# The product of ek and v on GpSimd instead of VectorE, one identity tile for all stages, and another head for the first mixing stage

## The reference

```
h   = layernorm(x) @ Wqkv + bqkv                    # 16 heads of 32
o   = softmax(q k^T / sqrt(32) + alibi bias) v
x   = x + o @ Wout + bout
emb = layernorm(x) + ctx
q, k, v = emb @ wq + bq, emb @ wk + bk, emb @ wv + bv
ek  = exp(k - max_t k);  ew = exp(w - max w)        # w: pos_bias within 128 of the diagonal, else 0
y   = sigmoid(q) * (ew @ (ek * v)) / (ew @ ek)
a   = layernorm(y @ wo + bo + emb) ...              # then a dense block of 512 -> 2048 -> 512 with relu
x   = x + layernorm(relu(a @ w1 + b1) @ w2 + b2 + a)
x   = x + quantised feed-forward with a depthwise convolution(layernorm(x))
```

## Time and profile before

| | |
|---|---|
| median of 3 runs | 3562.73 us (3561.97 to 3564.03) |
| the profiled execution | 3561.91 us |
| its span in the profile | 3560.3 us |
| PE busy | 3177.0 us, 89% |
| DVE busy | 2358.0 us, 66% |
| ACT busy | 1769.2 us, 50% |
| POOL busy | 1127.6 us, 32% |
| mean granted TensorE clock | 0.957 |

### The profile page before, as it was taken

How to read it: one execution, slowest core, us unless ns; L and a number is a source line. 1 busy time by engine, 2 the same in 40 slices (tenths; PEclk the granted TensorE clock), 3 DMA queues, 4 the chain that set the end, 5 groups by cost and what they waited for, 6 DMA issues and landing times. The chain is left out here.

```text
span 3560.3 us, 57155 instructions
## 1 busy us (share of the span) xinstructions
PE 3177.0 (89%) x19234; PEld 2286.5 (64%) x19234; DVE 2358.0 (66%) x4214; ACT 1769.2 (50%) x3131; POOL 1127.6 (32%) x892
## 2 busy tenths in 40 slices
PE   6998999999999999689996898599999999467887
PEld 5776666666666666467775777477887888334443
DVE  5562888888888888555553788634445444379996
ACT  3331888888888888412222222132222222066662
POOL 2343222311321231143331355311111111058886
PEclk9999999999999999889997999799999999689999
DMA  6775212211311222355644443321111110201112
GB/s 216 242 244 166 67 57 74 77 60 56 91 60 57 69 80 64 123 188 187 226 167 155 135 142 124 101 95 42 42 42 43 42 41 30 80 23 54 60 42 71
DMA packets 239608, 350.54 MB, mean 98 GB/s; under 512 B 31792, under 2 KB 129104, under 8 KB 239440
## 3 DMA queue, kind: packets, MB, share of 16 engines
q1 hardware_dynamic: 208784, 291.46, 25.3%
q0 software_dynamic: 8640, 31.77, 2.7%
q10 hardware_dynamic: 22016, 25.17, 2.0%
HBM read 210.68 MB, written 137.64 MB: 98 GB/s over the span
## 5 line engine op out<-in xcount | busy, mean ns | idle before, releaser
L863 DVE CUSTOM_DVE_ANT_0 attend_scores<-attend_scores,attend_bias_table 128x1024 f32<-128x1024 f32 x512 | 630.4, 1231 | 164.0 <-PE attend_scores L717 157.7
L790 ACT ACTIVATE attend_probs<-attend_scores,attend_neg_max 128x1024 f32<-128x1024 f32 x512 | 571.2, 1116 | 136.9 <-DVE attend_neg_max L863 126.8
L729 PE MATMUL attend_turned<-attend_ident,attend_probs 128*128 128x128 f32 x4096 | 557.5, 275 | 11.5 <-DVE attend_probsT L871 11.2
L729 PEld LDWEIGHTS attend_turned<-attend_ident,attend_probs 128*128 128x128 f32 x4096 | 473.0, 141 | 121.4 <-DVE attend_probsT L871 27.2
L717 PE MATMUL attend_scores<-attend_k_stack,attend_q_stack 96*128 96x512 f32 x1024 | 375.2, 448 | 14.4 <-DMA attend_q_stack<-qk_parts 9.8
L798 ACT COPY attend_probsT<-attend_turned 128x512 f32<-128x512 f32 x640 | 359.1, 583 | 25.4 <-PE attend_turned L729 23.5
L2207 DVE TENSOR_TENSOR cross_ffn_h_lo<-cross_ffn_hidden,cross_ffn_h_hi 128x512 fp32r<-128x512 f32 x128 | 96.3, 757 | 361.9 <-ACT cross_ffn_h_hi L2104 361.3
L691 POOL TENSOR_TENSOR attend_out_parts<-attend_out_full,attend_out_parts 128x256 fp32r<-128x256 f32 x64 | 46.5, 727 | 856.7 <-ACT attend_out_parts L805 856.7
L744 PE MATMUL attend_out_acc<-attend_probsT,attend_v_in 128*32 128x256 f32 x4096 | 312.9, 389 | 0.7 <-DVE attend_out_full L881 0.7
L871 DVE COPY attend_probsT<-attend_turned 128x512 f32<-128x512 f32 x384 | 263.4, 686 | 1.3 <-PE attend_turned L729 1.3
L717 PEld LDWEIGHTS attend_scores<-attend_k_stack,attend_q_stack 96*128 96x128 f32 x1024 | 154.1, 190 | 171.4 <-issue 169.2
(11 more groups left out here) (302 smaller groups left out, 6630.0 us busy)
## 6 DMA issues: line engine op xcount, KB each, us to landing
qk_parts<-qkv_qk_out SPq DMA_DIRECT2D x64, 512.0 KB, 3.2
attend_k_stack<-qk_parts SPq DMA_DIRECT2D x192, 128.0 KB, 2.5
attend_q_stack<-qk_parts SPq DMA_DIRECT2D x192, 128.0 KB, 2.6
qkv_wq_raw<-L_ffn_w POOLq DMA_DIRECT2D x16, 1024.0 KB, 7.8
o_parts<-attend_out_parts ACTq DMA_DIRECT2D x64, 256.0 KB, 2.5
mix_in_o_in<-o_parts SPq DMA_DIRECT2D x32, 512.0 KB, 6.7
qkv_x_in<-x SPq DMA_DIRECT2D x8, 1024.0 KB, 6.0
v_rows<-qkv_v_out SPq DMA_DIRECT2D x32, 256.0 KB, 3.4
```

Source lines behind the costliest of these rows:

```text
L729: last = pe.transpose(turned[:, x, c], probs[:, i % 2, k * P:(k + 1) * P], ident[:, :])
L790: act.activation(probs[:, i % 2], scores[:, i % 2], ACT.Exp, bias=neg_max[:, i % 4:i % 4 + 1], scale=-1.0, accum_out=den[:, qg % 2, j, h:h ...
L863: dve.tensor_tensor_reduce(scores[:, i % 2], scores[:, i % 2], bias_table[:, h, at:at + T], -1.0, BIG, ALU.add, ALU.min, neg_max[:, i % 4: ...
```

## The change

Four things are done together.

1. **The product of ek and v.** The four instructions leave VectorE's odd step and stand at the end of GpSimd's odd step, behind `mask_band`, `bias_x` and `embed`. VectorE keeps the sums and waits for each product (`ekv_ready`).
2. **One identity.** It is made once, in `project_qkv`, in a tile of the whole program. The five later stages take it and lose their memset, their select and TensorE's wait for them.
3. **Wout, o_in, x_in and the output bias go ahead.** They live in tiles that attention and `mix_in` share (`carried`). GpSimd issues the loads of Wout and of the bias as its first instructions of `attend` and splits Wout behind the tables of turn 0. SP loads `x_in` and `o_in` of half 0 behind the last turn's loads. GpSimd adds the bias to `x_in` before attention's last two low parts.
4. **The head of `mix_in`.** SP starts with the context, wk and wv. TensorE waits for nothing before its first products. VectorE does `residual_norm(0)` first and splits wk, wv and wq behind it. The wait for the four remaining bias loads comes late on every engine.

```diff
@@ attend, SP, behind the turns
+                def load_first():
+                    sp.wait_ge(wout_step, 2)
+                    sp.dma_start(first["x_in"][:, :, :], half_of(x, 0)).then_inc(x_loaded, 16)
+                    sp.wait_ge(out_stored, KB * G * 16)
+                    for g in range(KB):
+                        sp.dma_start(first["o_in"][:, g].bitcast(F32), o_parts[0, g, :, :, 0:HALF]).then_inc(first_loaded, 16)
+
                 turns(sp, body)
+                load_first()
+                sp.wait_ge(first_loaded, KB * 16)
@@ attend, GpSimd
+                pool.dma_start(first["x_in"][:, :, :], Wout.rearrange("(c p) n -> p c n", p=P)).then_inc(wout_loaded, 16)
+                pool.dma_start(first["bias"][:, :], row(bout, 0, D)).then_inc(wout_loaded, 16)
                 pool.iota(offsets[:, :], pattern=[[1, SPAN]], base=P - T, channel_multiplier=-1).then_inc(offsets_ready, 1)
...
-                identity(pool, ident[:, :], ident_step)
...
+                def split_wout():
+                    raw = first["x_in"][:, :, :]
+                    pool.wait_ge(wout_loaded, 32)
+                    pool.tensor_copy(first["w_hi"][:, :, :], raw).then_inc(wout_step, 1)
+                    pool.wait_ge(wout_step, 1)
+                    pool.tensor_tensor(first["w_lo"][:, :, :], raw, first["w_hi"][:, :, :].bitcast(F32), ALU.subtract).then_inc(wout_step, 1)
+
                 def body(turn):
                     tables(turn)
+                    if isinstance(turn, int) and turn == 0:
+                        split_wout()
...
                 turns(pool, body)
+                pool.wait_ge(x_loaded, 16)
+                for t in range(HT):
+                    pool.tensor_tensor(first["x_in"][:, t], first["x_in"][:, t], first["bias"][:, :], ALU.add).then_inc(x_biased, 1)
                 low_part(TURNS, 0)
                 low_part(TURNS, 1)
+                pool.wait_ge(x_biased, HT)
@@ mix_in, SP
-                sp.dma_start(w_raw[:, 0], SOURCES["out"].rearrange("(c p) n -> p c n", p=P)).then_inc(w_loaded[0], 16)
-                load(0, 0, 0)
-                sp.wait_ge(o_loaded, KB * 16)
                 load_ctx(0)
...
+                load_w(1)
+                load_w(2)
                 load(1, 0, 1)
+                load_w(3)
                 store(0)
                 load_ctx(1)
@@ mix_in, GpSimd
                 def step(n, h, more, b):
                     mask_band(n)
                     if more:
                         bias_x(n + 1)
                         embed(n + 1)
+                    if h == 1:
+                        for f in range(KB):
+                            pool.wait_ge(v_read, n * KB + f + 1)
+                            pool.wait_ge(ek_ready, b * KB + f + 1)
+                            pool.tensor_tensor(vT[:, f], vT[:, f], kT[:, f], ALU.mult).then_inc(ekv_ready, 1)
@@ mix_in, TensorE
-                pe.wait_ge(ident_step, 2)
...
-                    pe.wait_ge(o_loaded, (n + 1) * KB * 16)
+                    past(pe, o_loaded, n * KB * 16)
...
-                pe.wait_ge(w_lo_ready, 1)
                 out_products(0)
@@ mix_in, VectorE
                     if h == 1:
                         for f in range(KB):
-                            dve.wait_ge(v_read, n * KB + f + 1)
-                            dve.wait_ge(ek_ready, b * KB + f + 1)
-                            dve.tensor_tensor(vT[:, f], vT[:, f], kT[:, f], ALU.mult).then_inc(ekv_ready, 1)
-                        for f in range(KB):
                             dve.wait_ge(ekv_ready, b * KB + f + 1)
                             sum_tiles(1, f, vT)
 
-                dve.wait_ge(biases_loaded, 5 * 16)
-                split_w(0, "out")
+                residual_norm(0)
                 split_w(1, "k")
-                residual_norm(0)
+                split_emb(0, 0)
                 split_w(2, "v")
-                split_emb(0, 0)
                 split_w(3, "q")
+                dve.wait_ge(biases_loaded, 4 * 16)
                 steps(dve, step)
```

100 lines of the change are left out of this document (44 added, 56 removed).

## The result

The changed kernel takes **3542.34 us** (median of 5 runs, 3541.0 to 3547.39) against 3562.73 (5 runs): a ratio of 0.9947, 95% interval 0.9935 to 0.9958. Predicted were 3540.2. The profiled execution took 3542.3, with a span of 3540.7 and a mean granted clock of 0.962 (before 0.957). The total is near the forecast. Its terms are not all so near, and the experiments are mostly about that.

A forecast was written before the change was run, and what follows sets the result against it. No single bound: TensorE is busy in nearly every slice, with dips at stage borders. −19.9 + 2.0 − 4.3 + 3.3 − 3.6 = −22.5 takes 3561.9 to 3539.4, plus 0.8 for the median: 3540.2 us, range 3534 to 3549.

The forecast's parts named there:

- Head of the stage: First mixing stage: first product starts with the stage (15.9 us), VectorE's residual precedes wk's split (4.0): −19.9 us.
- Start of attention: Where Wout's loads were put: tables 1.35 us later, q and k loads share DMA: +2.0 us, ends +0.8 and +5.3.
- Products, odd steps: First mixing stage: three TensorE waits for VectorE's residual go, −4.3 us; e_far held behind GpSimd's product, +3.3 us.
- End of the stage: First mixing stage's end: products' 4.63 us leave VectorE, last split about 1.0 later: −3.6 us.
- Identity: Later stages: nothing gained, since each first transpose waits for a load that lands later.
- the second: Rival: 1.25 MB precede q and k loads (+3.3), e_far held longest, mixing start delayed: 3546.5 us, chance 0.25.
- the fourth: Rival: GpSimd bounds the odd step, measurable loss from 7.25 us a product, 3582 us at 8; chance 0.02.

The follow-up runs named there:

- e4: The changed kernel with SP's load of the first mask band moved right behind the first context load: 3536.2 us.
- e6: The changed kernel with the loads of Wout and the output bias issued by ScalarE instead of GpSimd, as its first instructions of attention: 3544.0 us.
- e1: The kernel before with only the four products of ek and v moved to GpSimd's odd step: 3554.7 us.
- e3: The changed kernel with the four products of ek and v put back on VectorE: 3550.9 us.
- e2: The kernel before with only the one identity tile for all stages: 3559.6 us, ratio 0.9995.
- e11: The changed kernel with the band's load early, Wout's load behind v's, and each GpSimd product cut into two of 128x512: 3534.6 us.
- e8: The changed kernel with every product done twice on GpSimd, first into a scratch tile: 3545.3 us.
- e7: The changed kernel with VectorE's small scaling of far behind the first q output instead of the third: 3546.1 us.
- e10: The changed kernel with the band's load early, Wout's load behind v's, and the scaling of far behind the first q output: 3533.2 us.
- e12: The changed kernel with the band's load early, Wout's load behind v's, and o_in last of the shared tiles: 3532.5 us.

## Why the prediction was right, and where it was not

1. **Head of the stage, −19.9.** To the transposes it was right: 45.83 − 26.40 = 19.4. The start came 16.0 earlier (15.9 said), the path from the first product to the aggregate is 3.4 shorter (4.0 said), and GpSimd's 7.5 are unchanged. What failed is what I put at nothing behind it: that the whole gain reaches the end of the stage, and that "wk, wv and wq arrive and are split ... as before". I followed the chain to the transposes and not SP's queue past it: the load of the first band, 52.6 us into the stage before, is now 39.9 into it, 12.7 earlier where TensorE came 19.4 earlier, since the stores ahead of it took 6.8 longer behind wq's load. What had been hidden became a wait of 6.4, and with the slow products behind it **8.8** were given back (e4). With the band's load moved the stage keeps the gain; whether wq's load moved would do the same was not tried. The low clock at the new start lasted until about 1487 (0.50, then 0.67 for 3 us), 4.4 us instead of the 2.9 that I took; in the eleven profiles that have this start it lasts 2.8 to 6.1 us. The rule that I had for this, to name what is late next, was not applied to the largest term.
2. **Start of attention, +2.0, was +3.6** (the six profiles with the load at the head against the eight without). The two parts were right in kind, but I took the score products as even with the tables and the sharing as equal. GpSimd's two issues took 1.33 (1.35 said), but it began them 0.48 behind SP's first load, so the iota starts 1.81 behind it and not 1.38, and the first table comes 1.6 later. That is hidden: the q and k loads of the first head were held 5.3 us (4.5 in e4), near my upper bound of 5.3, as if nearly all of the 1.25 MB had gone ahead of them. Without GpSimd's issues, in e6, the scores still come 4.6 later and attention is as long.
3. **Products, odd steps, −4.3 + 3.3 = −1.0, were −2.8** (three times 0.92, e1; in e3 it is 1.2 and 1.4 in steps 1 and 3, and −0.5 without its fall in step 5, where the wait did not come back). The three waits went. One product takes 2.4 (predicted 2.35), and TensorE's wait for `e_far` is 0.93 (1.1). What was missed is that this wait and the next one overlap: 0.4 come back in steps 1 and 3 (e1 against e2). The hold itself is shown by e11.
4. **End of the stage, −3.6, was −3.8**, in e1 as in the changed kernel.
5. **Identity, 0:** e2 agrees in the time; in the trace the start of attention gains 0.24.
6. **Not in the sum at all:** the output products went from 0.233 to 0.227 us apiece. A set of 48 takes 10.78 instead of 11.05 us from its first start to its last at the full clock, 0.27 for each of eight sets, so −2.2. And the profile before has two falls of the clock, that of the change none, 3.4 us by chance.

Worked out again with the measured terms: −19.4 + 8.8 + 3.6 − 2.8 − 3.8 − 2.2 − 3.4 = −19.2, against the −19.6 between the two profiled executions. This is no closer than its parts: the stage's terms make −22.8 where the stage measures −24.1, attention's 3.6 stand for 4.2 in this pair of profiles, and the other stages add 0.2. The forecast of −22.5 missed 0.5 + 8.8 + 1.6 = 10.9 on the one side and 1.8 + 0.2 + 2.2 + 3.4 = 7.6 on the other. That the total came within 2.1 us is luck: a term of 8.8 was missing, and others that I had not forecast made up for most of it. Of the rivals, the second had the right mechanism in its first part (the 1.25 MB ahead of q and k); the fourth, GpSimd as the bound, was as far off as it was put: at twice the duration (e8) it costs 2.4 us, all of it in the end of the stage.

## What to carry to other kernels

When a stage's start comes earlier, every engine's queue behind it has to come earlier by as much: list the loads that wait behind stores there and move up those that need no buffer. A load that is put at a quiet place of one engine can still stand ahead of a critical one in the DMA engines, whoever issues it. An instruction of VectorE that GpSimd's can hold is held for the rest of that one, so long GpSimd instructions can be cut, or the small one issued elsewhere. Both took TensorE's waits away here (e11, e7 and e10), and neither gained in the time; a wait that is taken away may be paid back by the clock, so look at the granted clock too.

## What was not expected of the hardware

- The same products, 128×128 by 512, run at 0.233 us apiece (median spacing 0.231 to 0.236 in the sets of before, e1 and e2) in one layout of the tiles and at 0.227 in another, in all eight sets of each of the eleven kernels that have it. It is not the work of VectorE (e3), not the identity's tile (e2), not the place of `o_in` (e12). Wout's tiles lie elsewhere in the changed kernel, which wasn't tried alone, so the cause stays open.
- TensorE's clock falls in the middle of a stage in which it is at work nearly all the time, behind an idle stretch of only 1.9 us among transposes, for 3.4 us each time and from none to six times in 400 us (e7, step 1, has the lines).
- 1.25 MB beside the loads of q and k held the first head of them for 4.5 to 5.3 us: nearly the time that the 1.25 MB take at the 236 GB/s of the earlier trace rows, and not the 3.3 of an equal share.
